# K of a long convolution in sets of 6, 8, 9 and 9 heads, the second set multiplied ahead of head 0, with two tiles taken up early and the last one finished in halves

## What is computed

```
# layer 0: a long convolution of each head, its kernel K made from 64 complex modes
dt = exp(log_dt);  A = -exp(log_A_real) + 1j*A_imag;  dtA = A * dt[:, None]
Ct = (C[..., 0] + 1j*C[..., 1]) * (exp(dtA) - 1) / A
K = 2 * einsum('hn,hnl->hl', Ct, exp(dtA[:, :, None] * arange(512))).real
y = causal_convolution(x, K) + x * D[:, None]
x = x + y * (arange(512)[None, :] < length[:, None])[:, None, :]
# layer 1: a linear layer with an adapter of rank 16, chosen by sample out of 32
A = lora_A_w[ids];  B = lora_B_w[ids]
x = x + (einsum('bsd,od->bso', x, base_weight) + base_bias) + (x @ A^T) @ B^T
```

## Time and profile before

| what | us |
|---|---|
| median of 3 runs | 215.61 (215.38 to 216.06) |
| the profiled execution: its own time | 214.99 |
| the profiled execution: span of the trace | 213.2 |
| TensorE busy | 192.8 |
| VectorE, ScalarE, GpSimd busy | 172.5, 114.9, 92.0 |
| transfers | 56.46 MB, 265 GB/s in the mean |

### The profile page before, as it was taken

The page is one execution under the profiler, slowest core; times in us unless marked ns, Lnnn a source line. Parts: engine busy times, 40 slices in busy tenths (PEclk is TensorE's granted clock), DMA queues, the critical chain, the costliest instruction groups (busy, mean ns, idle before and its releaser), DMA issues.

```text
span 213.2 us, 4331 instructions
## 1 busy us (share of the span) xinstructions
PE 192.8 (90%) x1047; PEld 165.8 (78%) x1047; DVE 172.5 (81%) x364; ACT 114.9 (54%) x330; POOL 92.0 (43%) x144
## 2 busy tenths in 40 slices
PE   0059999999989999699999999999999999999992
PEld 0047999998978999578888888888888888888881
DVE  4899498788799866979999978788887878788652
ACT  2747344433745326347667666657566565756430
POOL 4840000002575220989564654545454464545500
PEclk9999999999999999999999999999999999999999
DMA  5974999999999999856667667757776676764323
GB/s 125 306 302 144 386 398 337 400 414 408 409 411 410 408 409 418 352 171 193 215 234 256 222 212 211 231 192 208 205 235 199 217 219 199 243 181 168 108 105 131
DMA packets 21520, 56.46 MB, mean 265 GB/s; under 512 B 3394, under 2 KB 3842, under 8 KB 21250
## 3 DMA queue, kind: packets, MB, share of 16 engines
q1 hardware_dynamic: 18370, 47.78, 61.8%
q0 software_dynamic: 2560, 8.39, 13.6%
q10 hardware_dynamic: 576, 0.13, 0.3%
HBM read 45.64 MB, written 10.65 MB: 264 GB/s over the span
## 4 chain that ended last, share of the span: by engine, by line
PE 54%; DVE 1%; DVEq 0%; issue 0%; ACT 0%
PE k_ps L937 21%; PE y_ps L937 20%; PE z_ps L925 7%; PE y_ps L963 2%; PE y_ps L964 2%; PE k_ps L963 2%; PE k_ps L964 2%; DVE x_t L778 1%; DVEq L89 0%; DVE xp L782 0%; ACT xp L537 0%; DVE a_raw L817 0%
## 5 line engine op out<-in xcount | busy, mean ns | idle before, releaser
L902 PE MATMUL z_ps<-xp,strip 128*128 128x512 f32 (+3 forms) x384 | 64.3, 327 | 1.1 <-DMA strip<-k_pad 1.0
L902 PEld LDWEIGHTS z_ps<-xp,strip 128*128 128x128 f32 x384 | 59.4, 196 | 6.0 <-DMA strip<-k_pad 2.1
L937 PE MATMUL k_ps<-w_hi,xp 128*128 128x512 f32 x128 | 42.6, 393 | 0.0
L403 POOL CAST ag<-a_hl 128x128 fp32r x64 | 25.2, 397 | 39.8 <-PE z_ps L925 28.2
L408 POOL DMA_INDIRECT b_hl<-b_tab,b_idx x32 | 37.6, 1174 | 9.6 <-issue 9.0
L937 PE MATMUL y_ps<-w_hi,xp 128*128 128x512 f32 x120 | 39.9, 393 | 0.0
L529 ACT ACTIVATE ag<-a_hl 128x64 fp32r x128 | 25.5, 249 | 19.7 <-issue 19.6
L448 ACT ACTIVATE xp<-z_all 128x512 fp32r<-128x512 f32 x32 | 19.9, 629 | 24.2 <-PE z_ps L902 22.6
L727 DVE TENSOR_TENSOR xp<-z_all,xp 128x512 fp32r<-128x512 f32 x32 | 24.0, 755 | 4.9 <-ACT xp L448 4.7
L937 PEld LDWEIGHTS k_ps<-w_hi,xp 128*128 128x128 f32 x128 | 24.0, 188 | 4.8
L733 DVE TENSOR_TENSOR z_all<-z_ps,mask 128x512 f32<-128x512 f32 (+2 forms) x33 | 22.1, 669 | 6.4 <-PE z_ps L902 6.2
(11 more groups left out here) (122 smaller groups left out, 225.9 us busy)
## 6 DMA issues: line engine op xcount, KB each, us to landing
strip<-k_pad SPq DMA_DIRECT2D x31, 512.0 KB, 8.6
z_all<-x_conv SPq DMA_DIRECT2D x16, 512.0 KB, 10.0
x_t<-x_tile SPq DMA_DIRECT2D x32, 256.0 KB
out<-a_raw SPq DMA_DIRECT2D x32, 256.0 KB
a_raw<-a_t SPq DMA_DIRECT2D x2, 512.0 KB, 8.9
x_t<-b_rows SPq DMA_DIRECT2D x2, 512.0 KB, 10.8
w_sb<-w_t SPq DMA_DIRECT2D x2, 512.0 KB, 8.3
b_tab<-b_hl SPq DMA_DIRECT2D x1, 1024.0 KB, 10.6
```

Source lines behind the costliest of these rows:

```text
L403: last = g.tensor_copy(ag[:, s, :, :, q, :].rearrange("p c e r -> p e c r"), src)
L902: last = nc.tensor.matmul(z_ps[:, h % ZS, m * P:L], strip[:, h % SS, m * P:(m + 1) * P, t], xp[:, h % XS, 0:LC - m, e, :], start=(n == 0), ...
L937: last = nc.tensor.matmul(y_bank(s), xp[:, s % XS, c, e, :], w[:, c, :], start=(n == 0), stop=False)
```

## The change

K's sets become heads 0 to 5, 6 to 13, 14 to 22 and 23 to 31. TensorE multiplies the second set after 13 warming matmuls, runs three more and only then head 0. Heads 0 to 5 and head 6 have their exponentials taken one by one ahead of the loop, heads 7 to 13 in one operation whose arguments VectorE writes right after set 0's `scale`, and heads 14 to 31 one by one in ScalarE's loops 7 to 11, in each loop behind the sines. VectorE's `k_low(0)` comes before `phases` of set 1, and `k_low(1)` ahead of remainder 2. Pair 7 of x is loaded from ScalarE's queue right behind K's first store; the other loads of SyncE's loop shift by a head or so, and those of W come three heads sooner. W is rounded in loops 29 to 31 and once after the loop. Two tiles instead of one are taken up early. The last tile's base and adapter products are made in two halves of 256 columns, in two banks, with tile 30's adapter product between them, and its output is added and stored in halves. The id column comes with the table of lags, `zero` shares the memory of `h_b`, the work area has three buffers instead of four, and two additions of GpSimd stand later in its list.

The diff, cut:

```diff
@@ -53,8 +53,9 @@
-GROUPS = ((0, 8), (8, 16), (16, 24), (24, 32))
-G = 8
+GROUPS = ((0, 6), (6, 14), (14, 23), (23, 32))
+G = 9
+WS = 3
 NG = len(GROUPS)
 XS = 4
 SS = 6
@@ -68,23 +69,27 @@
 OS = XS
 AHEAD = 6
 EARLY = NH - 2
+EARLY_T = 2
 NW = 4
 PRE = 7
-X_AT = {5: 7, 7: 8, 10: 9, 13: 10, 15: 11, 17: 12, 19: 13, 21: 14, 23: 15}
-IDS_AT = 6
-A_AT, B_AT, W_AT = {9: 0, 12: 1}, {16: 0, 18: 1}, {27: 0, 29: 1}
+X_AT = {6: 8, 8: 9, 12: 10, 14: 11, 16: 12, 18: 13, 20: 14, 22: 15}
+IDS_AT = 7
+A_AT, B_AT, W_AT = {10: 0, 13: 1}, {15: 0, 17: 1}, {24: 0, 26: 1}
 XT_AT = 30
 SPLIT_A = {17: 0, 18: 1, 19: 2, 20: 3}
-SPLIT_B = {21: 0, 22: 1, 23: 2, 24: 3}
-K_AFTER = {1: 0, 2: 7, 3: 14}
-WARM = 15
+SPLIT_B = {22: 0, 23: 1, 24: 2, 25: 3}
+SPLIT_W = {29: 0, 30: 1, 31: 2}
+K_AFTER = {2: 7, 3: 14}
+WARM_0, WARM_1 = 13, 3
+MAG_FIRST = 7
+MAGS_AT = {7: (14, 18), 8: (18, 23), 9: (23, 26), 10: (26, 29), 11: (29, 32)}
 STEPS_AT = {2: (4, 5, 6, 7, 8, 9), 3: (10, 11, 12, 13, 14, 15)}
...
@@ -238,13 +243,13 @@
             sp.dma_start(par[:, :, :], params).then_inc(par_in, 16)
             sp.dma_start(tab[:, :], table).then_inc(table_in, 16)
-            sp.dma_start(d_sb[:, :], d_row).then_inc(d_in, 16)
             load_pair(0)
             load_pair(1)
+            sp.dma_start(d_sb[:, :], d_row).then_inc(d_in, 16)
             sp.wait_ge(zeroed, 1)
             sp.dma_start(k_pad[:, 0:P, :].rearrange("h (o p) e -> h o (p e)", o=2),
-                         zero[0:NH, :].unsqueeze(1).to_broadcast((NH, 2, P))).then_inc(pad_stored, 16)
-            sp.dma_start(len_sb[:, :], length.to_broadcast((P, NB))).then_inc(len_in, 16)
+                         zero[0:NH].unsqueeze(1).to_broadcast((NH, 2, P))).then_inc(pad_stored, 16)
+            sp.dma_start(len_sb[:, :], length).then_inc(len_in, 16)
             for n in range(2, PRE):
                 load_pair(n)
...
@@ -308,10 +312,15 @@
             with sp.Fori(2, NT // OS) as lap:
                 for s in range(OS):
                     pass_tile(lap * OS + s, s)
-            for t in range(NT - AHEAD, NT):
+            for t in range(NT - AHEAD, NT - 1):
                 store(t, t % OS)
+            for n in range(2):
+                cols = slice(n * L // 2, (n + 1) * L // 2)
+                sp.wait_ge(o_done, NT + n)
+                rows_of = out.rearrange("(t b h) l -> t h b l", b=BT, h=NH)[NT - 1:NT, :, :, cols]
+                sp.dma_start(rows_of.rearrange("o h b l -> (o h) b l"), o_sb[:, OS - 1, cols]).then_inc(stored[OS - 1], 16)
             for s in range(OS):
-                sp.wait_ge(stored[s], 16 * (NT // OS))
+                sp.wait_ge(stored[s], 16 * (NT // OS + s // (OS - 1)))
...
@@ -351,8 +360,6 @@
             link(g.tensor_tensor(sm[:, 4:6, :], par[:, 2:4, :], twice(ea[:, :]), ALU.mult))
             link(g.tensor_tensor(mm[:, 0, 0, :], sm[:, 4, :], sm[:, 6, :], ALU.subtract))
             link(g.tensor_tensor(mm[:, 0, 1, :], sm[:, 5, :], sm[:, 7, :], ALU.add))
-            link(g.tensor_tensor(mm[:, 1, 1, :], sm[:, 6, :], sm[:, 4, :], ALU.subtract))
-            link(g.tensor_tensor(mm[:, 1, 0, :], sm[:, 5, :], sm[:, 7, :], ALU.add))
             pool.wait_ge(th_ready, 1)
             g.tensor_scalar(rc[:, 1, :], th[:, :], -1.0, 1.0, ALU.mult, ALU.add).then_inc(rc_ready, 1)
             pool.wait_ge(rc_ready, 1)
@@ -363,6 +370,8 @@
             g.tensor_tensor(cs_x[:, 0, :], an[:, 0, :], turn, ALU.add).then_inc(angle_ready, 1)
             pool.wait_ge(rec_ready, 1)
             g.tensor_tensor(ez[:, :], th_1[:, :], rr[:, 1, :], ALU.mult).then_inc(ez_ready, 1)
+            link(g.tensor_tensor(mm[:, 1, 1, :], sm[:, 6, :], sm[:, 4, :], ALU.subtract))
+            link(g.tensor_tensor(mm[:, 1, 0, :], sm[:, 5, :], sm[:, 7, :], ALU.add))
             four = mm[:, :, :, :].rearrange("p o t h -> p (o t) h")
             g.tensor_tensor(four, four, rr[:, 0, :].unsqueeze(1).to_broadcast((P, 4, NH)), ALU.mult).then_inc(scaled, 1)
...
             act.wait_ge(table_in, 16)
-            for h in range(GROUPS[0][1]):
-                act.activation(mag[:, h, :], tab[:, 0:NL], ACT.Exp, scale=zr[:, h:h + 1]).then_inc(mags, 1)
+            def magnitudes_of(h0, h1):
+                for h in range(h0, h1):
+                    act.activation(mag[:, h, :], tab[:, 0:NL], ACT.Exp, scale=zr[:, h:h + 1]).then_inc(mags, 1)
+            magnitudes_of(0, GROUPS[0][1])
             act.wait_ge(angle_ready, 1)
             act.activation(cs[:, :, :], cs_x[:, :, :], ACT.Sin, scale=SMALL_TURN).then_inc(cs_ready, 1)
             group_sines(0)
             split_x(0)
+            magnitudes_of(GROUPS[1][0], MAG_FIRST)
+            group_store(0)
+            act.dma_start(z_all[:, PRE * XP:(PRE + 1) * XP, :, :].rearrange("p h c b -> p h (c b)"),
+                          x_conv[:, PRE * XP:(PRE + 1) * XP, :]).then_inc(x_landed[PRE], 16)
+            magnitudes(MAG_FIRST, GROUPS[1][1], 1)
+            group_sines(1)
             split_x(1)
-            group_store(0)
-            group_sines(1)
-            magnitudes(GROUPS[1][0], NH, 1)
             split_x(2)
+            group_store(1)
             split_x(3)
             for h in range(XS, NH):
...
@@ -505,6 +528,8 @@
                 for k, at in STEPS_AT.items():
                     if h == at[3]:
                         group_sines(k)
+                if h in MAGS_AT:
+                    magnitudes_of(*MAGS_AT[h])
...
+                if h in SPLIT_W:
+                    split_w(SPLIT_W[h])
             def gather(t, s):
...
+            def part_rounded(t, h0, h1, done):
+                act.activation(by_head(xp[:, t, :, 0, :], h0, h1), by_head(in_chunks(x_t[:, t, :]), h0, h1),
+                               ACT.Copy).then_inc(done, 1)
+            split_w(NW - 1)
             gather(0, 0)
             gather(1, 1)
-            split_w(0)
-            split_w(1)
-            act.wait_ge(x1_early, 1)
-            act.activation(by_head(xp[:, 0, :, 0, :], 0, EARLY), by_head(in_chunks(x_t[:, 0, :]), 0, EARLY),
-                           ACT.Copy).then_inc(xhi_early, 1)
-            split_w(2)
-            split_w(3)
-            act.wait_ge(x1_done, 1)
-            act.activation(by_head(xp[:, 0, :, 0, :], EARLY, NH), by_head(in_chunks(x_t[:, 0, :]), EARLY, NH),
-                           ACT.Copy).then_inc(xhi_done, 1)
-            x1_hi(1, 1, True)
+            for t in range(EARLY_T):
+                act.wait_ge(x1_early, t + 1)
+                part_rounded(t, 0, EARLY, xhi_early)
+            for t in range(EARLY_T):
+                act.wait_ge(x1_done, t + 1)
+                part_rounded(t, EARLY, NH, xhi_done)
+            x1_hi(2, 2, True)
             h_down(0, 0)
             h_rounded(0, 0, True)
-            x1_hi(2, 2, True)
             gather(2, 0)
             for i in range(0, 2):
...
@@ -694,7 +718,7 @@
                     link(V.tensor_tensor(gg[:, s, 0:n, :], g2[:, 0:n, 0, :], g2[:, 0:n, 1, :], ALU.add))
                 def scale():
-                    dve.wait_ge(mags, GROUPS[0][1] + min(k, 1))
+                    dve.wait_ge(mags, h1 if k == 0 else MAG_FIRST + 1 + h1 - GROUPS[1][1])
...
@@ -744,17 +768,18 @@
             coefficients()
             multiply()
             scale()
+            exponents_of(MAG_FIRST, GROUPS[1][1])
             turns, phases, whole, fraction, multiply, scale = group(1)
             turns()
+            k_low(0)
             phases()
             whole()
-            k_low(0)
             fraction()
-            exponents_of(GROUPS[1][0], NH)
             remainder(0)
-            remainder(1)
             multiply()
             scale()
+            remainder(1)
+            k_low(1)
             remainder(2)
             remainder(3)
...
@@ -814,8 +839,15 @@
                         dve.wait_ge(bias_in, 16)
                     if not known or i - 1 >= OS:
                         dve.wait_ge(stored[(s - 1) % OS], 16 * (lap + (s - 1) // OS))
-                    V.tensor_tensor(o_sb[:, (s - 1) % OS, :], y_bank(s - 1), bias_sb[:, :],
-                                    ALU.add).then_inc(o_done, 1)
+                    if known and i == NT:
+                        for n in range(2):
+                            cols = slice(n * L // 2, (n + 1) * L // 2)
+                            dve.wait_ge(y_done, NT + n)
+                            V.tensor_tensor(o_sb[:, OS - 1, cols], y_bank(YS - 1 + n)[:, 0:L // 2], bias_sb[:, cols],
+                                            ALU.add).then_inc(o_done, 1)
+                    else:
+                        V.tensor_tensor(o_sb[:, (s - 1) % OS, :], y_bank(s - 1), bias_sb[:, :],
+                                        ALU.add).then_inc(o_done, 1)
...
             for h in range(NH - XS, EARLY):
                 head(h)
+            dve.wait_ge(z_masked, EARLY)
             dve.wait_ge(xt_landed[0], 16)
-            dve.wait_ge(z_masked, EARLY)
-            part_of_x1(0, EARLY, x1_early)
+            part_of_x1(0, 0, EARLY, x1_early)
```

(58 more changed lines are left out.)

51 lines of the change are left out of this document (26 added, 25 removed).

## The result

The changed kernel takes 217.15 us in the median of 19 runs (215.99 to 218.5), the kernel before 215.85 in 19 runs beside it. The ratio is 1.0064, 95% interval 1.0047 to 1.008: 0.6% slower, where 0.2% faster was forecast (215.1, with 214.2 to 216.2 for the forecast's own case and 213.0 to 216.9 for 8 in 10). The profiled execution took 216.69, its span 214.5. Span against span that is 1.3 us more than before; the forecast had 0.55 less. In the changed kernel L937 is a head's matmul, L918 and L920 are K's, L909 is the warming, L260 loads a strip, L233 a pair of x, L238 a half of A, B or W, L492 stores K, L514 is pair 7 on ScalarE's queue, L976 is the base product of a tile.

The account below looks back on a forecast made before the run. Transfers were taken to set the pace until strip 20, then TensorE. Transfers +1.15, change of stage -0.85 and end -0.85 sum to -0.55: 214.45 us profiled, 215.1 median; range 214.2 to 216.2, 213.0 to 216.9 for 8 in 10.

Parts of the forecast that it names:

- cost nothing, bound 0.5: At the start, pair 7's load on ScalarE's queue uses idle transfers: no cost, 0.5 us if it delays strip 0.
- ScalarE's loop: Loop 7's sines, table load and exponentials make TensorE wait 1.8 us before set 2; bounds 0 and 2.5.
- Rival A: ScalarE's lag doesn't reach set 2's `scale`, so its store leaves on time: sum -2.15, 213.5 us; chance 0.33.
- rival D: Table switches before head 0 and in loop 7 hold ScalarE another 1.28 us each: 217.7 us; chance 0.02.
- The transfers: Up to strip 19, two SyncE waits for K's stores leave transfers idle; head 20 and convolution's end 1.15 us later.
- rival B: K's two stores wait longer in the queue, 6.85 us, shifting everything behind by 1.35: 216.4 us; chance 0.12.
- Idle: 1.0: Transfers idle 1.0 us before strip 6, which waits for the second set's store; bounds 0 and 2.
- Idle: 1.6: Transfers idle 1.6 us before strip 14, which waits for set 2's store; bounds 0 and 2.9.
- W's loads: W three heads sooner puts two more loads ahead of strips 25 and 27, landing 0.4 us early: no cost.
- Change of stage: Between convolution and tile 1, earlier W rounding gains 0.85 us; bounds 0.6 lost and 1.2 gained.
- Rival C: No gain at the change of stage, GpSimd's W remainders running past convolution's end: 215.9 or 216.5 us; chance 0.13.
- End: After the last matmul, the last tile in column halves gains 0.85 us; bounds 0.4 and 1.2.

Follow-up runs that it names:

- experiment 6: The changed kernel with K's sets of eight heads again and the single exponentials redistributed over loops 7 to 11 to suit: 213.16 us, ratio 0.9864.
- experiment 2: The changed kernel with pair 7 loaded by SyncE behind strip 5 again, not from ScalarE's queue: 215.62 us, ratio 1.0.
- experiment 7: Experiment 4 with pair 7 loaded from ScalarE's queue behind K's first store: 216.26 us, ratio 1.0024.
- experiment 1: The changed kernel with the single exponentials of heads 14 to 31 in loops 4 to 6 instead of 7 to 11: 215.45 us, ratio 0.9988.
- experiment 5: The changed kernel with the edits of experiments 1 and 2 together: 215.05 us, ratio 0.9956.
- experiment 3: The changed kernel with pairs 14 and 15 behind strips 21 and 23 instead of 20 and 22: 217.01 us, ratio 1.0064.
- experiment 4: The kernel before with the late parts alone: W sooner and rounded in the loop, two tiles taken up early, last tile in halves: 214.54 us, ratio 0.9938.
- experiment 8: Experiment 6 with single exponentials in loops 4 to 6 and pair 7 on SyncE's queue behind strip 5: 212.6 us, ratio 0.9853.
- experiment 9: Experiment 4 with an unused array of 512 B per partition in front of the strips and other arrays: 214.87 us, ratio 0.9941.
- experiment 11: Experiment 8 with B's halves loaded behind strips 19 and 21 instead of 15 and 17, rounded two loops later: 212.69 us, ratio 0.9852.

## Why the prediction was wrong

**What bounds the kernel: right.** Transfers set the pace up to the strips near head 20, in every experiment but the sixth, where TensorE, late at head 1 and held for 1.18 before set 2, never caught up with them.

**The start: the time of head 0 right, one term wrong.** Set 0's store left at 14.62 (forecast 14.75), the strips at 16.30 (16.5), set 1's matmuls at 19.48 (19.45), head 0 at 20.75 (20.85). The step that failed here is "cost nothing, bound 0.5" for pair 7. Its ground, that the transfers stood idle there, was one microsecond (17 to 18) before strip 0's first bytes. Pair 7 kept the transfers busy past it: TensorE now waits inside head 0 and ahead of head 1. From 18.0 to 27.6 the rate was 326 GB/s, as before (329), though the strips were issued 1.0 sooner. Experiments 2 and 7 price it: 0.6% and 0.9% of the time, 1.4 and 1.9 us. The bound was set below the 1.28 that one load of 512 KB takes; nothing in the trace excluded that or more.

**ScalarE's loop: right, somewhat large.** The wait was 1.39, against 1.8, and ran through sines, table load and exponentials as worked out. Experiment 1 shows the cause. The first tiles put its price at 0.7 us (experiment 1 against the changed kernel) and 0.9 (5 against 2), the ratios at 0.8% and 0.4%. Rival A fell with it. The table load lasted 1.28 (32.75) and the exponential began at 34.04. By the rule of the Trainium skill's page "ScalarE: Activation LUTs", section "What ACT_TABLE_LOAD costs", another 1.38 us of drain would have put it at 35.4; the trace does not agree, and rival D fell.

**The transfers: the step that failed.** Both waits of SyncE came, at the forecast places. Set 1's store landed after 6.4 us (forecast 5.8) and set 2's after 5.7 (5.5), so rival B's 6.85 at both did not come. What failed is the count of the stream up to strip 19. Head 19 waits for this strip in both kernels, so the rows give the time from the issue of the strips to it: 48.75 us (16.30 to 65.05) where it was 44.32 (17.27 to 61.59). That is 4.4 more, where the forecast had 1.0 + 1.6 = 2.6. Two of its terms fell short:

- Pair 7, "cost nothing". Pair 13 took its place in SyncE's order, so this stretch holds one load more than before (pair 7 left at 15.01 and landed 3.6 later), up to 1.28 us at full rate.
- "Idle: 1.0" and "Idle: 1.6". The idle time was right, but I counted the queue as moving at 410 GB/s as soon as a strip's first bytes came, and it took four us more to get there. Instead of 2.6 us, 2.3 + 2.6 were lost, less the 1.1 that the kernel before lost too: 3.8.

Together they are up to 2.5 us too small, which more than covers the 1.8 that are missing; the runs don't part the two exactly. The strips went out 0.2 sooner than forecast, and head 19 came at 65.05 instead of 63.35, 1.7 late.

Experiment 6 undoes the sizes, with the exponentials split to suit: both slow stretches vanish, SyncE waits 1.2 us for K instead of 9.9, and the time falls from 1.0064 to 0.9864, by more than the forecast had charged for all transfers. With sets of 8 the first strip of a set stands three or four loads further from its set's store: strips 6 and 7, pair 8 and in some kernels pair 7 lie ahead of strip 8, and not of strip 6. SyncE waited 4.9 us for K in the kernel before too, and no idle stretch followed; that distance hid the landing.

**W's loads: right by their own count. Head 23: not foreseen.** "Land 0.4 before they are needed; nothing" was said of strips 25 and 27, and no head after 23 waits. The wait of 1.15 is for strip 23, and W's first half was issued behind strip 24, at 65.03. By issue and time to landing, strip 22 lands at 70.1 (59.54 + 10.6), pair 15 at 72.8 (59.90 + 12.9) and strip 23 at 74.1 (62.08 + 12.0). Loads come 1.28 apart, so pair 15 is 1.4 late, and without that strip 23 would have been in time. From 69.8 on one of the 16 DMA engines was held by a transfer of instructions. This is its row in the view of the DMA queues from 69 to 70 us, with packets, MB and the share of 16 engines; 6.8% are 1.1 us of one:

```profile
q8 instruction: 1, 0.02, 6.8%
```

Each of the thirteen traces has such a transfer between 66 and 72 us. A load came 0.25 to 1.4 us late behind it in eight of them, and none did in five. So this cause is likely and not shown. In experiment 3 strip 23 stood ahead of pair 15, and waits came at heads 24 and 25 instead. The end of convolution is 89.05 + 1.7 + 1.15 = 91.9 (measured 91.8 by the weight loads, 91.9 by the matmuls).

**Change of stage: right.** First matmul 1.6 after the convolution's end; the small operations took 0.15 to 0.18 instead of 0.95; tile 1's first product at +4.95 (forecast +4.85). Rival C fell.

**End: nearly right.** From the last matmul's end to the end of the span it is 3.06 us (214.5 less 211.44) where it was 3.76: a gain of 0.7, against 0.85.

**Tiles: not foreseen.** A period of 3.673 us instead of 3.713 gave back 1.2 us over 30 tiles. The sum of the profiled spans closes: 2.75 (convolution) + 0.1 (tile 1) + 0.15 (end) - 1.2 (tiles) = 1.8, of the 1.85 from the forecast's 212.65 to 214.5. The remaining 0.2 of 2.05 between the medians, 215.1 and 217.15, is how the medians lie to the profiled spans. Without that gift, which is luck as far as the prediction goes, the change would have been 1.2% slower.

The measured 217.15 lies nearest to rival D's 217.7; that is chance, since its pause at the table load didn't come.

Pair 7 and ScalarE's lag cost 0.6% and 0.8% apart and 1.1% together (experiment 5). Whether they add isn't settled: each ratio is known to 0.2%, and by the first tiles they do (1.5 and 0.7 us apart, 2.4 together). The late parts gained the 0.6% of experiment 4. Against it, K's part with everything repaired (experiment 8) gains 0.9%: 0.4 us up to the first tile (1.6 against the profile of experiment 9), and 1.2 us of tile pace whose cause stays open.

## What to carry to other kernels

Where a load waits for a small store, count how many loads of the queue lie between the two, and keep them longer than the store's slowest landing; uneven sets move that point, and a set that starts sooner may leave its successor nothing to hide behind. Here a queue that ran dry cost about twice its idle time (2.3 and 2.6 us for 1.0 and 1.5), since the rate came back over several microseconds. When a load is moved into idle time, count it in the stream all the same. Bandwidth that looks idle right ahead of the first load that an engine waits for isn't free, and where transfers set the pace, changing the order of loads moved waits and won no time (experiments 3 and 11).

## What the runs showed of the hardware

- After a dry stretch the rate rose over about four us: 184, 283, 365 GB/s in steps of 2 us in the changed kernel from 48 to 54, each behind issues that stood in the queue, with the DMA share at 0.73, 0.92 and 1.03. In the kernel before it fell to 326 and 264 from 34 to 38 at a share of 1.00 and 0.99, with no dry stretch ahead.
- One 512 KB load from another queue, issued 1.4 us ahead of the first strip, moved that strip's first use by 1.76 us (experiments 4 and 7; 1.69 against experiment 9), more than the 1.28 that such a load takes at full rate.
- Of the four stores of K of the changed kernel, 24 to 36 KB each, the first took 1.6 us to land, and the others, behind busy queues, 6.4, 5.7 and 5.6.
- 512-column matmuls of the tile stage took 390 ns in the mean in kernels with K's new part and 393 in the others, at a granted clock of 1.0 in both. It repeats in all eleven experiments. Moving the arrays by 512 B didn't change it (experiment 9); other differences (code, the smaller work area, the column in the table) weren't tried apart.
- Experiments 4 and 9 differ in nothing but that unused array, and their medians agree (214.54 and 214.87), yet head 14 waited 0.23 in one profile and 1.28 in the other. The load of x ahead of its strip, issued at 37.47 and 37.55, took 11.0 us to land in one and 12.0 in the other. A single profile doesn't price a microsecond of waiting.
- A transfer of instructions (queue q8) held one of 16 DMA engines for 1.0 to 1.1 us near 70 us in every trace; in eight of thirteen a load behind it landed 0.25 to 1.4 us late.
